# The causal mask of an attention block becomes constant rows of the query and key stacks

## What is computed

```python
x = token ids [32, 128];  h = weight[x]                      # D = 256
h = h + attention(layernorm(h))                              # 16 heads of 16, 32 sequences of 128
# scores = q k^T / 4, scores[q, s] = -inf where s > q, softmax over s, times v, output projection
h = h + ffn(layernorm(h))                                    # top 1 of 8 experts, capacity 641 rows
# expert: gelu(x W1 + b1) W2 + b2, F = 1024, weighted with the softmax of the router
```

## Time and profile before

| | |
|---|---|
| median of 3 runs | 621.98 us (621.16 to 622.57) |
| profiled execution | 621.5 us, of which the span is 619.6 us |
| TensorE busy | 581.8 us, 94% |
| VectorE busy | 418.6 us, 68% |
| ScalarE busy | 346.2 us, 56% |
| GpSimd busy | 258.5 us, 42% |

### The profile page before, as it was taken

How to read it: one execution, slowest core, us unless ns; L and a number is a source line. 1 busy time by engine, 2 the same in 40 slices (tenths; PEclk the granted TensorE clock), 3 DMA queues, 4 the chain that set the end, 5 groups by cost and what they waited for, 6 DMA issues and landing times.

```text
span 619.6 us, 14358 instructions
## 1 busy us (share of the span) xinstructions
PE 581.8 (94%) x5357; PEld 498.1 (80%) x5357; DVE 418.6 (68%) x1073; ACT 346.2 (56%) x708; POOL 258.5 (42%) x316
## 2 busy tenths in 40 slices
PE   5878999999999999999998899999999999999991
PEld 3557677877787777787665499999999999999990
DVE  7335678988898888888766656575756565656521
ACT  2314555565555556555462386767676767676720
POOL 5536777765566665555563300303030303030303
PEclk9977999999999999999999999999999999999996
DMA  4687876756777644556111350333332333320101
GB/s 125 162 270 211 268 238 211 237 164 207 244 243 222 199 147 129 155 163 224 36 37 69 96 164 1 106 111 106 113 114 103 108 107 102 112 80 2 34 1 32
DMA packets 42821, 84.39 MB, mean 136 GB/s; under 512 B 6846, under 2 KB 33011, under 8 KB 39104
## 3 DMA queue, kind: packets, MB, share of 16 engines
q1 hardware_dynamic: 35840, 70.66, 36.5%
q0 software_dynamic: 6144, 12.67, 6.7%
q10 hardware_dynamic: 768, 0.13, 0.1%
HBM read 52.64 MB, written 31.74 MB: 136 GB/s over the span
## 4 chain that ended last, share of the span: by engine, by line
PE 83%; DVE 7%; DMA 4%; issue 2%; POOL 2%; ACT 1%; POOLq 0%; SPq 0%; ACTq 0%; DVEq 0%
PE M L602 14%; PE M L1192 9%; PE S L1175 9%; PE PV L1192 9%; PE C L1175 9%; PE PV L752 6%; PE S L631 6%; PE C L648 4%; PE S L634 4%; PE M L554 3%; PE M L617 2%; PE M L711 2%; PE C L1142 2%; DMA ks<-k_parts 2%; PE M L1130 1%
## 5 line engine op out<-in xcount | busy, mean ns | idle before, releaser
L1053 POOL DMA_INDIRECT out_dram<-ys,xs x48 | 50.7, 1057 | 212.3 <-DVE ys L1244 202.6
L432 POOL TENSOR_SCALAR_AFFINE_SELECT pt<-pt 128x512 f32<-128x512 f32 x128 | 81.4, 637 | 81.3 <-ACT pt L473 80.3
L473 ACT ACTIVATE pt<-C 128x512 f32<-128x512 f32 x128 | 76.4, 597 | 65.5 <-PE C L648 63.4
L832 DVE TENSOR_REDUCE mx<-S 128x4 f32<-128x512 f32 x128 | 86.6, 681 | 7.7 <-PE S L634 7.2
L1257 DVE TENSOR_TENSOR hl<-gl,hh 128x324 fp32r<-128x324 f32 x128 | 63.4, 496 | 37.3 <-ACT hh L1093 37.0
L1093 ACT ACTIVATE hh<-gl 128x324 fp32r<-128x324 f32 x128 | 59.2, 469 | 0.0
L631 PE MATMUL S<-maskb,identb 128*128 128x512 bf16 x128 | 51.2, 400 | 7.3 <-DMA ks<-k_parts 6.2
L752 PE MATMUL PV<-pt,va 128*32 128x128 f32 x1024 | 54.1, 285 | 0.9 <-ACT os L480 0.8
L634 PEld LDWEIGHTS S<-ks,qs 96*128 96x128 bf16 x512 | 40.8, 99 | 16.2 <-issue 1.8
L634 PE MATMUL S<-ks,qs 96*128 96x128 bf16 x512 | 51.1, 223 | 0.0
L648 PE MATMUL C<-qs,ks 97*128 97x128 bf16 x512 | 50.3, 220 | 0.1
(11 more groups left out here) (165 smaller groups left out, 1702.8 us busy)
## 6 DMA issues: line engine op xcount, KB each, us to landing
w_raw<-in_L_ffn_W_dram SPq DMA_DIRECT2D x16, 1024.0 KB, 9.0
qs<-q_parts SPq DMA_DIRECT2D x48, 256.0 KB, 4.2
ks<-k_parts SPq DMA_DIRECT2D x48, 256.0 KB, 5.2
q_parts<-qp SPq DMA_DIRECT2D x16, 384.0 KB, 2.5
k_parts<-kp SPq DMA_DIRECT2D x16, 384.0 KB, 2.7
rows_of_slots<-w_raw SPq DMA_DIRECT2D x6, 877.5 KB, 8.3
xs<-rows_of_slots SPq DMA_DIRECT2D x7, 658.1 KB
out_dram<-h SPq DMA_DIRECT2D x16, 256.0 KB, 5.3
```

The source lines that it names most:

```text
L432: pool.affine_select(out=buf[:, :, :], in_=buf[:, :, :], compare_op=ALU.is_ge, fill=0.0, base=0, pattern=[[0, 4], [1, S]], channel_multipl ...
L473: act.activation(pt[u % 4][:, :, :], bC[u % 2][:, :].rearrange("p (j t) -> p j t", j=4), ACT.Exp, scale=SCALE).then_inc(a_exp, 1)
L832: dve.tensor_reduce(mx[g.slot][:, 4 * (u % QUADS):4 * (u % QUADS) + 4, u // QUADS], bS[u % 2][:, :].rearrange("p (j t) -> p j t", j=4), AX ...
```

## The change

The mask product of a unit goes. Instead rows 97 to 127 of `ks` and `qs` hold constants whose products add up to a huge negative number above the diagonal and to nothing on and below it; the maxima's product reads 128 rows in place of 96, and row 96 of `qs`, which holds the previous group's maxima by then, is set to zero before it. The `C` product reads the same 97 rows as before.

GpSimd makes the two patterns (`kmask`, `qmask`, 128x128) with two memsets and twelve selects, each select waiting for the one before it on the same tile. ScalarE spreads each over eight copies (into `x2t` and `xn2`, which are still free), and SyncE's queue copies them into the four ring slots: slots 0 and 1 before step 0, slot 2 in step 1, slot 3 in step 2. From step 4 on a small DMA in each step zeroes row 96 of `qs`. The identity in bf16 and its copy go, `maskb` becomes `constb` (ones, for the idle products), and one select of 128x512 at the start goes. The weights of experts 0 and 1 come in quarters in the steps 7 to 14. GpSimd's two stores of a group go one place later each.

```diff
+Q_MASK = tuple(2.0 ** e for e in (116, 90, 64, 38, 12))
+K_MASK = tuple(-(2.0 ** e) for e in (-93, -67, -41, -15, 11))
...
-            sp.wait_ge(v_ones, 1)
-            for i in range(RING):
-                sp.dma_start(ks[i][KS_ROWS:KS_ROWS + 1, :, :], onesb[0:H * GT // P, :]).then_inc(d_ones, 16)
...
+            def fixed_rows(i):
+
+                for stack, rows_of, more in ((ks[i], kmask8, 1), (qs[i], qmask8, 2)):
+                    sp.wait_ge(a_mask, more)
+                    sp.dma_start(stack[KS_ROWS:, :, :].rearrange("p h t -> p (h t)").rearrange(
+                                     "p (a c) -> p a c", c=MASKS * S),
+                                 rows_of.unsqueeze(1).to_broadcast([P - KS_ROWS, H * GT // S // MASKS, MASKS * S])
+                                 ).then_inc(d_fixed[i], 16)
+
+            fixed_rows(0)
+            fixed_rows(1)
...
                     hold(sp, pe_C, g.back(RING - 1).times(UNITS))
+                    if g.off >= RING:
+                        sp.dma_start(qs[g.slot][KS_ROWS:KS_ROWS + 1, :, :], qmask[0:H * GT // P, :]).then_inc(d_zero[g.slot], 16)
...
+                if 1 <= i < RING - 1:
+                    fixed_rows(i + 1)
...
-                if BLANKS < i <= BLANKS + 4:
-                    e, half = divmod(i - BLANKS - 1, 2)
-                    load_half[half](sp, e, e)
+                if BLANKS < i <= BLANKS + 4 * KC:
+                    e, quarter = divmod(i - BLANKS - 1, 2 * KC)
+                    load_half[quarter // KC](sp, e, e, quarter % KC)
...
+            def mask_rows():
+
+
+                per, at = len(Q_MASK), KS_ROWS + 1
+                pool.memset(kmask[:, :], K_MASK[-1]).then_inc(p_kmask, 1)
+                pool.memset(qmask[:, :], Q_MASK[-1]).then_inc(p_qmask, 1)
+                for n, c in enumerate(range(per - 1, -1, -1)):
+                    pool.wait_ge(p_kmask, n + 1)
+                    pool.affine_select(out=kmask[:, :], in_=kmask[:, :], compare_op=ALU.is_ge,
+                                       fill=K_MASK[c - 1] if c else 0.0, base=per * at - c - 1, pattern=[[1, S]],
+                                       channel_multiplier=-per).then_inc(p_kmask, 1)
...
             pool.tensor_tensor(rs1[:, :], ve1[:, :], halfneg[:, 0:GB], ALU.pow).then_inc(p_rs1, 1)
+            mask_rows()
             for g in gathers[:1]:
                 gather(g)
...
+            def spread_rows():
+
+                for dst, src, done in ((kmask8, kmask, p_kmask), (qmask8, qmask, p_qmask)):
+                    act.wait_ge(done, len(Q_MASK) + 2)
+                    act.activation(dst.rearrange("p (a t) -> p a t", t=S),
+                                   src[KS_ROWS:, :].unsqueeze(1).to_broadcast([P - KS_ROWS, MASKS, S]), ACT.Copy
+                                   ).then_inc(a_mask, 1)
...
                     from_bank(xth, bM0, pe_T, g0, a_xth)
+                if i == 0:
+                    spread_rows()
```

More of the change, by code:

```diff
@@ L183, in attention_phase @@
     SPREAD = E * SL // 96 // BLANKS
+    MASKS = 8
     Q_PAIRS = ((0, 0), (1, 2), (0, 1))
@@ L239, in attention_phase @@
         x2t = sb("x2t", [P, KC, GT], F32)
+        kmask8, qmask8 = (t[KS_ROWS:, :, :].rearrange("p a b -> p (a b)").bitcast(BF16) for t in (x2t, xn2))
         lmax = sb("lmax", [P, GB], F32)
@@ L261, in attention_phase @@
         g_set, g_cst, v_cst = sem("g_set"), sem("g_cst"), sem("v_cst")
+        p_qmask, p_kmask, a_mask = sem("p_qmask"), sem("p_kmask"), sem("a_mask")
+        d_zero, d_fixed = ([sem(f"{n}{i}") for i in range(RING)] for n in ("d_zero", "d_fixed"))
         v_xf, pe_id, v_idt, pe_w, a_wh, v_wl = (sem(n) for n in ("v_xf", "pe_id", "v_idt", "pe_w", "a_wh", "v_wl"))
@@ L409, in gather @@
                                             ).then_inc(d_g[g % RING], 16)
+            def mask_rows():
[7 more added lines that the diff above has]
+                                       channel_multiplier=-per).then_inc(p_kmask, 1)
+                pool.wait_ge(p_kmask, per + 1)
+                pool.affine_select(out=kmask[:, :], in_=kmask[:, :], compare_op=ALU.is_ge, fill=1.0, base=-at,
+                                   pattern=[[0, S]], channel_multiplier=1).then_inc(p_kmask, 1)
+                for n, c in enumerate(range(per - 1, -1, -1)):
+                    pool.wait_ge(p_qmask, n + 1)
+                    pool.affine_select(out=qmask[:, :], in_=qmask[:, :], compare_op=ALU.is_ge,
+                                       fill=Q_MASK[c - 1] if c else 0.0, base=per * at - c, pattern=[[1, S]],
+                                       channel_multiplier=-per).then_inc(p_qmask, 1)
+                pool.wait_ge(p_qmask, per + 1)
+                pool.affine_select(out=qmask[:, :], in_=qmask[:, :], compare_op=ALU.is_ge, fill=0.0,
+                                   base=per - 1 - per * at, pattern=[[-1, S]], channel_multiplier=per
+                                   ).then_inc(p_qmask, 1)
             gathers = list(range(NG))
@@ L535, in step @@
                         wait(act, pe_lg, g5.times(1))
+                    if g5.off == 0:
+                        for ring in d_fixed:
+                            act.wait_ge(ring, 32)
                     from_bank(x2t, turn_bank(g5), pe_x2T, g5, a_x2t)
@@ L560, in idle_work @@
                 for _ in range(count):
-                    pe.matmul(bank[:, :], trib[:, :], maskb[:, :, :], start=True, stop=True)
+                    pe.matmul(bank[:, :], trib[:, :], constb[:, :, :], start=True, stop=True)
             FILL = {(1, 1): 6, (1, 4): 18, (NG + 3, 1): 4, (NG + 3, 3): 3, (NG + 3, 5): 6, (NG + 3, 6): 3,
@@ L628, in step @@
                             wait(pe, d_k[g.slot], g.round(48, 48))
+                            wait(pe, d_fixed[g.slot], 32)
+                            wait(pe, d_zero[g.slot], g.round(16))
                         dst, b = bS[u % 2], u // QUADS
                         wait(pe, v_mx, g.times(UNITS, u - 1))
-                        pe.matmul(dst[:, :], identb[:, :], maskb[:, :, :], start=True, stop=False)
                         for j in range(4):
@@ L862, in second_norm @@
                         wait(dve, p_rs2, g.times(1, 1))
+                        if g.off == 0:
+                            for ring in d_fixed:
+                                dve.wait_ge(ring, 32)
                         dve.tensor_copy(h[:, bass.ds(g.times(GB), GB), D + 1:D + 3], mv2[:, :, :])
@@ L1037, in step @@
                     for load in load_half:
-                        load(sp, e2.times(1), e2.slot)
+                        for k in range(KC):
+                            load(sp, e2.times(1), e2.slot, k)
                     for j in range(NT):
@@ L1149, in idle_work @@
                 for _ in range(count):
-                    pe.matmul(bPV[:, :], trib[:, :], maskb[:, :, :], start=True, stop=True)
+                    pe.matmul(bPV[:, :], trib[:, :], constb[:, :, :], start=True, stop=True)
             for r in range(TURNS - 1):
```

68 lines of the change are left out of this document (32 added, 36 removed).

## The result

| | before | after |
|---|---|---|
| median, us | 622.19 (620.10 to 624.26, 11 runs) | 626.57 (623.46 to 629.89, 11 runs) |
| ratio, 95% interval | 1 | 1.0064 (1.0038 to 1.0091) |
| span of the profiled execution | 619.6 | 622.3 |
| VectorE `kr` of group 5 to `kr` of group 15 | 182.78 | 182.51 |
| `kr` of group 15 to the last COPY of the attention phase | 60.93 | 64.23 |

The account below looks back on a forecast made before the run. It took a ring of waits between VectorE and TensorE, not TensorE's sum, as the bound in the attention phase. 621.5 - 12.4 (gains) + 2.4 (start) + 0.5 (constant rows) = 612.0 us; range 603 to 617.

Parts of the forecast that it names:

- What costs nothing: Part of the prediction giving no cost to the zero row, quarters, later stores and the 128x512 select at the start.
- The ring of waits: VectorE and TensorE hand work over once a full step; 0.58 us a step gained, 5.8 in ten steps.
- the rival of 602 us: Full steps shrink to VectorE's own work, or COPY drops from 1.14 to 0.16 us; time about 602, chance 0.15.
- The rival of a falling clock: TensorE's clock falls in the steps as it idles; one slow step costs 15 us, 627 or more, chance 0.06.
- The start: GpSimd's patterns delay group 0's work by 2.4 us (bounds 1.2 and 4.4), with selects taken at 0.35.
- The spreads: ScalarE's two 32x1024 copies at the start, about 1 us each, claimed to be covered by the late qr.
- The DMA wait ahead of group 1's scores: Named as a sign of being wrong; constant rows were given 0.5 us, bounds 0 and 3.
- The gains ahead of group 5 and in the tail: Mask products removed outside the ten full steps: 1.6 + 0.9 + 2.3 + 1.8 = 6.6 us.
- the 12.4 of gains: All savings from removing the mask product: 5.8 us in ten full steps and 6.6 in the steps around them.

Follow-up runs that it names:

- e1: The kernel after with GpSimd's two stores back at places 4 and 6: 615.91 us, ratio 0.9883 to the kernel before.
- e3: The kernel after with one idle product of constants ahead of each unit's scores behind the last group: 624.97 us, ratio 1.0029.
- e4: The kernel after with stores back at places 4 and 6 and idle products behind the last group: 616.24 us, ratio 0.9898.
- e8: The kernel before without the mask product and without constant rows, the mask left out of the maxima: 612.51 us, ratio 0.9869.
- e9: The kernel after with GpSimd's first store moved back, so stores at places 4 and 7: 619.46 us, ratio 0.9961.
- e2: The kernel before with only GpSimd's two stores moved to places 5 and 7, mask product kept: 626.53 us, ratio 1.0057.
- e6: The kernel after with stores back at places 4 and 6 and the selects of kmask and qmask alternated: 612.94 us, ratio 0.9875.
- e10: The kernel after with GpSimd's second store moved back, so stores at places 5 and 6: 621.84 us, ratio 1.0005.

## Why the prediction was wrong

**The step that failed** is in "What costs nothing": "The stores one place later: GpSimd idles at those places." It looked at GpSimd's own time, which the stores do not lengthen, and not at VectorE's instructions beside it. The runs put it at 8.7 to 11.5 us. By e1 it is 10.7 in the medians (626.57 and 615.91), and 11.5 with each against the before of its own group (622.19 and 623.06); e3 and e4, in one group, differ by 8.7. In the profiled executions of the kernel after and e1 it is 5.4 in the ten steps and 3.9 in the tail, 9.3. It turned the sign, and the forecast had no rival for it: "slower" was held for TensorE's clock alone.

**The ring of waits was right.** Full steps of 17.61 (forecast 17.66) in e1 and in e8, ten steps shorter by 5.7 (5.8). In the kernel after the wait for `kr` is 0.87 (1.09 less 0.22) and TensorE idles for VectorE ahead of Q: 0.41 in the row above, where I had some 0.8. The reading of TensorE's full 182.75 of 182.78 us as the bound would have given 18 us in ten steps. COPY stayed at 1.15, as I expected, so the rival of 602 us did not come. The rival of a falling clock came in one step of one trace, e9's, and cost about 1 us there and not 15, since the clock was back at 1.00 from 133 us on, well before the step's end at 135.72.

**The other terms.** The start was mis-sized: selects at 0.42 and not 0.35, `rs1` of group 1 later by 2.78 and not 2.4. The spreads hid, as forecast; each took 1.05. The DMA wait ahead of group 1's scores, which the forecast had named as a sign of being wrong, came. It was longer than the 0.5 that I took: 1.20 us in the kernel after, and 2.84 in e1, near the bound of 3. e1 has another wait, of 2.78, ahead of a `C` product for the transfer of `nm`, which the forecast did not count; e8, without constant rows, has 1.33 there. The DMA share is 0.95 in 46 to 52, where the earlier trace rows have 0.00 in 46 to 48:

```profile
49.93 0.38 PE L688 MATMUL S<-ks,qs 128*128 128x128 bf16 x4 [1.20 <-DMA ks<-k_parts]
```

The gains ahead of group 5 and in the tail were sized too high. I had 4.8 by the `kr` of group 5; e8, which has no start cost from selects or constant rows, has 2.75 (95.62 to 92.87), and e2, which keeps the mask product, came at 93.47 in its one execution, so that the gain could be as little as 0.6. I had 1.8 in the tail; e8 has 0.2. Taken together e8's 8.6 us (621.10 to 612.51) stand against the 12.4 of gains. The costs of the start do not show in full in the medians: e6's `kr` of group 5 comes 2.05 us later than e8's (94.92 and 92.87), its tail is 0.6 shorter, at the full clock, and its profiled execution is 1.4 longer (613.83 and 612.43), but the medians differ by only 0.4 (612.94 and 612.51). With six runs each that is not resolved.

So 612.0 is wrong for the change as it was made. That it lies within 1 us of e6, the change with its stores left in place and its selects interleaved, is partly luck: the gains were 3.8 too high, and the forecast had the chained selects. With these and the early stores the change gave 7.2 us (e1) where the sum had 9.5. By terms, 8.7 to 11.5 of the 14.6 us are the stores; the rest lies in the over-sized gains and the start, and the runs do not part these more finely.

## What to carry to other kernels

When an instruction moves on GpSimd, read which VectorE instructions lie beside its new place, and not only whether GpSimd is idle there: a 128x16 operation went from 0.17 to 0.68 us in each of the last eight full steps. Count what each engine between two waits loses, since a step in which VectorE hardly waits passes such a loss on in full (0.49 for 0.48 in e9, 0.71 for 0.72 in e1). In the kernel before, a loss of 0.15 left the step as it was. A loss of the size of the changed kernel's was not tried there.

## What the runs showed of the hardware

**A store by GpSimd holds VectorE, but not always.** Beside the indirect store, `oh` took 0.17 us in e2, whose store starts 0.32 to 0.34 ahead of it, and 0.67 or 0.68 in the kernel after at the same distances, in all of the last eight full steps of each; in e9, 0.44 ahead, it took 0.65 in two of them and 0.17 or 0.18 in six. e2's rows:

```profile
178.51 1.03 POOL L398 DMA_INDIRECT rows_of_slots<-h,pos  x1 [0.19 <-issue]
178.83 0.17 DVE L934 TENSOR_TENSOR oh<-iota,first 128x16 bf16<-128x16 f32 x1
```

When it is long it ends within 0.05 us of the store's end, so it is held up beside the store. The recorded distance alone does not decide whether `oh` gets by; what does stays open. The Trainium skill, SBUF — State Buffer, on the shared port pair, says that a VectorE instruction with two inputs in SBUF is blocked by a GpSimd instruction that reads SBUF, for its whole length; e10's `oh` beside the select agrees (0.58, ending 0.02 after it). The same page infers that such an operation is not in the way of descriptor writing; the 0.68 of the kernel after speaks against that, if the write of descriptors is what the store does in that time, which no run here separates from its read of the index column.

**A chain of dependent selects on GpSimd** of 128x128 costs 0.42 us a link. Two chains interleaved cost 0.25 to 0.26 an instruction, but for one, at 0.32.

**TensorE's clock falls after short waits too.** In e8 TensorE waited 0.74 us at 294.55 and 0.64 at 295.81, and its granted clock was 0.50 from 297 to 299, that is 1.2 GHz, and 1.00 again from 300 to 309. e9's step above is the same with waits of 0.80 and 0.41. The tails at a clock of 0.94 are the 0.4 to 0.8 us longer.

**The added rows of a product cost next to nothing:** a score product of 128 rows took 0.225 us in the mean, one of 96 rows 0.223, and ten steps 177.07 and 177.04.
